# Normalizing with tokens on the partitions: transposes and row statistics in place of matrix products, in a four-layer attention and feed-forward kernel

## The chip, the cores and the metric

One NeuronCore of a Trainium2 chip runs the whole program in one launch. The metric is the device time in microseconds. The engines are PE (TensorE, matrix products; its weight loads are shown apart as PEld), DVE (VectorE), ACT (ScalarE), POOL (GpSimd) and SP (SyncE, which here only issues DMAs). Each engine works through its own instruction queue in order and waits on semaphores that the others raise.

## The reference

The input is 2 batches of 2048 tokens with 128 features. Four blocks follow, each with its own weights, and then an outer norm, a feed-forward part with ternary weights, and a last norm:

```
for i in range(4):
    residual = x
    q, k, v = x @ Wq[i] + bq[i], x @ Wk[i] + bk[i], x @ Wv[i] + bv[i]
    Q, K = elu(q) + 1, elu(k) + 1
    KV, Ksum = sum over tokens of K * v, sum over tokens of K
    V = Q * KV * 1 / (Q * Ksum + 1e-6)
    a = gelu(gelu(V @ Wo[i] + bo[i]))
    x = ln(a + residual) * ln1_s[i] + ln1_b[i]          # norm "1"
    residual = x
    f = gelu(gelu(x @ W1[i] + b1[i]) @ W2[i] + b2[i])    # 128 -> 512 -> 128
    x = ln(f + residual) * ln2_s[i] + ln2_b[i]           # norm "2"
x = layernorm(x_in + x)                                  # norm "x"
h = gelu_exact(x @ ternary(W_fc)); h = layernorm(h) * ln_w + ln_b   # over 512, norm "g"
x = layernorm(x + h @ ternary(W_proj))                   # norm "z"
```

Every norm takes mean and variance over the features of one token.

## The kernel before

Everything on chip is kept transposed: the 128 features lie on the 128 partitions and the tokens run along the free dimension. The 4096 tokens are cut into four pairs of 1024 (`PAIR`, two PSUM banks), two pairs p = 0, 1 for each batch n. PSUM is four tiles of 128x1024, handed out in the fixed order of the list `ORDER` (in the tail `TURNS`).

The work goes in 8 steps (t = 0 to 7; a step is one batch in one layer, batches in turn, so layer 0 is steps 0 and 1), followed by a tail. Step t does the attention of its batch, norm 1 and the up product with its gelu; beside them it does what the step before left over for the other batch: the down product, its gelu and norm 2. So a step waits at its start for the norm 2 that the step before finished last. Matrix products with weights that need more precision are made of three single-pass products (`xh*wh`, `xh*wl`, `xl*wh`: lines 957, 958, 963), where `xh` is x rounded to fp32r and `xl` the remainder. The plain fp32 products show as two records each in the profile (so `x8` for 4 matmuls).

A norm in this layout sums over partitions, which only PE does here:

1. `centered` (L880 for norms 1, x, z; L883 and L885 for norm 2, from `xh`, `xl` of y): the product with I - 1/128 gives y minus its mean in PSUM.
2. ACT squares it (L326) and copies it to `yc` (L327).
3. `mean_rows` (L892): 8 products for a pair with one column of 1/128, in turn in another place of the weights, put the variances of 8x128 tokens into an 8x128 (or 16x128) tile.
4. DVE runs `rsqrt_of` on that tile (L486 to L511, 11 instructions, each waiting for the one before).
5. `spread` (L899): 8 products with `pick` spread the result over all partitions.
6. DVE multiplies with scale and rstd (L693, L680, L518), adds the shift (L699, L682, L524), and `xh` and `xl` are made for the next product (L394, L409, L521 and L533, L298).

The order on PE in a step is: k, v, q products of both pairs; down product of the other batch's pair 0; attention output; half of the down product of pair 1; norm 1 of both pairs with norm 2 of pair 0 between; up products of pair 0; up products of pair 1 with norm 2 of pair 1 between. The tail does norm 2 of the last batch, norm x, the 512-wide hidden layer with the exact gelu (L1122, L1124, L437), its norm g from sums that DVE (L803), ACT (L447) and POOL (L311, L316) make, the projection (L1109) and norm z, for the four pairs, and stores the output transposed back on the host.

SP stores each pair when its norm z is done. POOL makes the remainder `xl` of y (L290) for norm 2 and of x (L298).

## Time and profile before

| | |
|---|---|
| three timed runs | 651.79, 648.50, 651.72 us; median 651.72 |
| span of the profiled execution | 649.9 us (its time outside the span isn't recorded) |
| PE | 570.2 us busy (88%), 2436 matmul records |
| DVE | 460.4 us (71%), 807 instructions |
| ACT | 380.4 us (59%), 371 |
| POOL | 116.6 us (18%), 62 |
| mean granted TensorE clock | 0.967 of full speed |

The span is measured from the first instruction to the last of one execution. Busy time is the sum of the records of an engine. PE records are modelled at their ends and overlap, so the time that a row of matmuls takes is best read from the starts of its rows. In a row of the timeline the number in brackets is the idle time of that engine before it, with what ended it.

### The profile page before, as it was taken

To read this page: it belongs to the slowest core of one execution; us is meant where nothing else is said; L and a number is where in the kernel's file an instruction comes from. 1 tells how busy PE (TensorE), PEld (TensorE's weight loads), DVE (VectorE), ACT (ScalarE), POOL (GpSimd) and SP (SyncE) were. 2 spreads that over 40 slices of the span, in tenths; PEclk is the share of its full clock that TensorE was granted. 3 is DMA by queue.
4 is the path that set the end of the run, shared out by engine and by line. 5 is a ranking of instruction groups with operands and counts; after the bars stand their busy time and mean duration, and the time that the engine had idled before them with its cause. 6 is when DMAs were issued, how large, how long until landed. Compare 5 with 4: busy or idle time off the path is not lost.

```text
span 649.9 us, 7136 instructions
## 1 busy us (share of the span) xinstructions
PE 570.2 (88%) x2436; PEld 358.0 (55%) x2436; DVE 460.4 (71%) x807; ACT 380.4 (59%) x371; POOL 116.6 (18%) x62
## 2 busy tenths in 40 slices
PE   4687989988998899989898988998899989894995
PEld 3345635753674466456645653675366565662554
DVE  6856466886678497758766987579477286989644
ACT  2653774767586747766774777476745348237030
POOL 6200010311021112011300311021110119018000
PEclk9877999999999999999999999999999989997997
DMA  6000100000001000000100000000001010000003
GB/s 210 0 2 0 49 2 0 2 0 1 2 0 49 0 0 0 0 0 0 48 1 0 0 0 0 0 0 0 2 0 66 1 65 2 1 0 2 0 1 129
DMA packets 2756, 10.26 MB, mean 16 GB/s; under 512 B 560, under 2 KB 560, under 8 KB 2480
## 3 DMA queue, kind: packets, MB, share of 16 engines
q1 hardware_dynamic: 2736, 9.99, 4.4%
q8 instruction: 12, 0.20, 0.1%
q14 instruction: 8, 0.07, 0.0%
HBM read 7.90 MB, written 2.10 MB: 15 GB/s over the span
## 4 chain that ended last, share of the span: by engine, by line
PE 49%; DVE 31%; issue 10%; ACT 9%; DMA 0%; DVEq 0%; ACTq 0%; SPq 0%
PE tile L892 13%; PE tile L880 6%; PE tile L899 6%; PE tile L1109 5%; PE tile L957 5%; PE tile L963 4%; PE tile L958 4%; DVE y L712 4%; DVE kk L615 3%; DVE kw L609 3%; DVE a L803 2%; DVE y L624 2%; DVE qw L622 2%; ACT y L348 1%; ACT a L384 1%
## 5 line engine op out<-in xcount | busy, mean ns | idle before, releaser
L957 PE MATMUL tile<-xh,wh 128*128 128x512 f32 x224 | 97.0, 433 | 19.2 <-DVE xh L750 9.5
L984 PE MATMUL tile<-h,w 128*128 128x512 f32 x224 | 101.6, 601 | 4.1 <-ACT a L367 2.0
L290 POOL TENSOR_TENSOR xl<-y,xh 128x1024 fp32r<-128x1024 f32 x16 | 38.1, 2381 | 358.4 <-DVE xh L529 358.4
L963 PE MATMUL tile<-xl,wh 128*128 128x512 f32 x224 | 89.0, 409 | 4.6 <-POOL xl L298 4.6
L958 PE MATMUL tile<-xh,wl 128*128 128x512 f32 x224 | 90.5, 404 | 0.0
L373 ACT ACTIVATE h<-tile,b 128x1024 f32<-128x1024 f32 x64 | 69.5, 1109 | 33.9 <-PE tile L963 33.8
L892 PE MATMUL tile<-sq,slide 128*16 128x128 f32 (+1 forms) x640 | 74.9, 276 | 0.0
L984 PEld LDWEIGHTS tile<-h,w 128*128 128x128 f32 x224 | 40.8, 190 | 56.8 <-issue 48.5
L892 PEld LDWEIGHTS tile<-sq,slide 128*16 128x16 f32 (+1 forms) x640 | 59.6, 95 | 19.3 <-ACT yc L327 5.3
L957 PEld LDWEIGHTS tile<-xh,wh 128*128 128x128 f32 x224 | 43.2, 193 | 44.5 <-issue 14.5
L326 ACT ACTIVATE sq<-tile 128x1024 f32<-128x1024 f32 x40 | 41.3, 1032 | 41.2 <-PE tile L880 37.6
L880 PE MATMUL tile<-y,center 128*128 128x512 f32 x96 | 48.7, 638 | 18.1 <-DVE y L712 15.1
L899 PE MATMUL tile<-rr,pick 48*128 48x128 f32 (+1 forms) x352 | 49.7, 286 | 12.6 <-DVE rr L511 12.5
L899 PEld LDWEIGHTS tile<-rr,pick 48*128 48x128 f32 (+1 forms) x352 | 44.4, 196 | 27.5 <-issue 24.6
L394 ACT ACTIVATE xh<-yc,att 128x512 fp32r<-128x512 f32 (+1 forms) x24 | 20.7, 862 | 57.2 <-DVE yc L693 57.2
L963 PEld LDWEIGHTS tile<-xl,wh 128*128 128x128 f32 x224 | 42.8, 194 | 19.4 <-POOL xl L298 7.3
L958 PEld LDWEIGHTS tile<-xh,wl 128*128 128x128 f32 x224 | 43.5, 194 | 7.3
L486 DVE TENSOR_SCALAR vv<-tile 8x128 f32<-8x128 f32 (+1 forms) x28 | 7.8, 278 | 51.9 <-PE tile L892 51.7
L298 POOL TENSOR_TENSOR xl<-x,xh 128x1024 fp32r<-128x1024 f32 x12 | 30.1, 2512 | 75.7 <-DVE x L524 44.8
L327 ACT ACTIVATE yc<-tile 128x1024 f32<-128x1024 f32 x40 | 41.5, 1038 | 0.0
L880 PEld LDWEIGHTS tile<-y,center 128*128 128x128 f32 x96 | 18.2, 201 | 41.8 <-issue 39.8
L712 DVE TENSOR_TENSOR y<-a,x 128x1024 f32<-128x1024 f32 x16 | 34.0, 2158 | 6.6 <-ACT a L384 5.6
(138 smaller groups left out, 927.1 us busy)
## 6 DMA issues: line engine op xcount, KB each, us to landing
raw<-layers SPq DMA_DIRECT2D x3, 774.5 KB, 4.2
x<-x_t SPq DMA_DIRECT2D x4, 512.0 KB, 6.7
y<-x_t SPq DMA_DIRECT2D x2, 1024.0 KB, 5.1
out_t<-x SPq DMA_DIRECT2D x4, 512.0 KB, 2.6
raw<-layers SPq DMA_DIRECT2D x1, 512.0 KB, 7.6
raw<-layers SPq DMA_DIRECT2D x1, 256.0 KB, 2.6
sq<-fc_t SPq DMA_DIRECT2D x1, 256.0 KB, 7.1
sq<-proj_t SPq DMA_DIRECT2D x1, 256.0 KB, 7.3
```

The source lines that it names most:

```text
L290: pool.tensor_tensor(xl[:, c], y[:, c], xh[:, c].bitcast(F32), ALU.subtract).then_inc(y_lo["2"], 1)
L326: act.activation(squares_of[k][:, p, :], tile[slot][:, :], ACT.Square).then_inc(sq_ready[k], 1)
L327: act.activation(yc[:, cols(n, p)], tile[slot][:, :], ACT.Copy).then_inc(yc_ready[k], 1)
L373: act.activation(h[:, p, j * PAIR:(j + 1) * PAIR], tile[slot_of(("h", p, j))][:, :], ACT.Gelu_apprx_tanh, bias=b1[:, j:j + 1]).then_inc(h_ ...
L712: dve.tensor_tensor(y[:, cols(n, p)], a1[:, p, :], x[:, cols(n, p)], ALU.add).then_inc(y_ready["1"], 1)
L880: mm = pe.matmul(dst, center[:, :].bitcast(F32), y[:, c], start=True, stop=True)
L892: mm = pe.matmul(dst, weights[:, at:at + rows], src[:, r * ROW:(r + 1) * ROW], start=first and r == 0, stop=last and r == ROWS_PER_PAIR - 1)
L899: mm = pe.matmul(tile[slot][:, r * ROW:(r + 1) * ROW], pick[0:LOW + rows, row0 + r, :], rr, start=True, stop=True)
L957: pe.matmul(dst, wh[:, w0:w0 + P], xh[:, c], start=True, stop=False)
L958: pe.matmul(dst, wl[:, w0:w0 + P], xh[:, c], start=False, stop=False)
L963: mm = pe.matmul(dst, wh[:, w0:w0 + P], xl[:, c], start=False, stop=True)
L984: mm = pe.matmul(dst, w2[:, j * P:(j + 1) * P], h[:, p, j * PAIR + at:j * PAIR + at + BANK], start=(j == 0), stop=(j == FT - 1))
```

## The change

In all norms the tokens go to the partitions. `turned` transposes eight 128x128 blocks of a pair with PE's transpose into PSUM (identity as the moving operand). In that layout a token's 128 features lie in one partition's row: DVE takes `bn_stats` of each block (8 instructions of 128 columns for a pair), and `moments` makes mean, variance, 1/sqrt and -mean/sqrt for the 8 blocks at once with 16 small instructions of 128x8 elements. The normalized rows `nt` are made from PSUM block by block (128x128) by DVE (`rows_normed`, subtract and multiply) or ACT (Identity with scale and bias), transposed back by PE, and scale and shift of the norm are applied on the way out of PSUM by ACT (for pair 1 of norm 2 by DVE). The squares, the products with `center`, `slide` and `pick`, and the POOL work for y are gone. PSUM slots are given out by the lists `USERS`.

In the tail the hidden layer comes out in rows as well: `hidden(m)` makes 256 tokens x 512 features with the tokens on the partitions (16 chunks, m = 0 to 15), ACT applies the exact gelu into `hd`, DVE takes `bn_stats` of 512 columns twice, `hidden_turned` transposes 8 blocks back for the projection (128x128 products), and the projection comes out in rows. Its norm's 1/sqrt is then a scalar for each row, applied in `final_sum` with the residual rows `nt` (to which POOL has added the constant part, `with_constant`). Norm z needs no transposes, and the output is stored in rows in eight pieces of 512 columns. The last norm 2 is applied together with the sum for norm x (`outer_sum`), for which POOL adds the shift to the input (`shifted`).

```
...
-TURNS += [("rf", 3), ("cz", 1), ("vz", 0), ("cz", 2), ("cz", 3), ("rz", 0), ("rz", 1), ("vz", 1), ("rz", 2), ("rz", 3)]
-LAST = [key for key in TURNS if key[0][-1] != "+"]
+MEAN, RSTD, SHIFT, VAR, A, B, C = range(7)
+NCOLS = 7
+MOMENT_STEPS = 16
+HIDDEN_STEPS = 13
+NEWTON_SCALE = 0.375 ** 0.2
+
+
+USERS = [[("k", 0), ("v", 1), ("o", 1), ("n2", 0), ("h", 1, 2)],
+         [("v", 0), ("q", 1), ("n1", 0), ("h", 0, 1), ("h", 0, 3), ("h", 1, 1)],
+         [("q", 0), ("f", 0), ("f", 1), ("h", 0, 0), ("h", 0, 2), ("h", 1, 0), ("h", 1, 3)],
+         [("k", 1), ("fold", 0), ("o", 0), ("n1", 1), ("n2", 1)]]
+OF_STEP_BEFORE = ("f", "n2")
+CHUNKS = FT
 
 
...
-            def squares(k, slot, n, p, done, reuse=None):
-
-                act.wait_ge(c_mm[k], done + 1)
-                if reuse is not None:
-                    act.wait_ge(var_mm[k], reuse)
-                act.activation(squares_of[k][:, p, :], tile[slot][:, :], ACT.Square).then_inc(sq_ready[k], 1)
-                act.activation(yc[:, cols(n, p)], tile[slot][:, :], ACT.Copy).then_inc(yc_ready[k], 1)
+            def affine(dst, src, scale, shift, done):
+                act.activation(dst, src, ACT.Identity, bias=shift, scale=scale).then_inc(done, 1)
+
+            def rows_normed(k, slot, n, p, q, rows):
+
+                for r in rows:
+                    last = act.activation(nt[:, row_cols(n, p, r)], tile[slot][:, r * P:(r + 1) * P], ACT.Identity,
+                                          bias=value(k, q, SHIFT, r), scale=value(k, q, RSTD, r))
+                last.then_inc(n_act[k], 1)
...
+            def moments(k, q, call, eps, width=P):
+
+                base = call * MOMENT_STEPS
+                done = moment[k]
+                even, odd, even2, odd2 = (stats[k][:, q, :, c] for c in (1, 4, 2, 5))
+                mean, shift, rstd, v, a, b, c = (value(k, q, z) for z in (MEAN, SHIFT, RSTD, VAR, A, B, C))
+                dve.wait_ge(stats_ready[k], call + 1)
+                dve.tensor_tensor(a, even, odd, ALU.subtract).then_inc(done, 1)
+                dve.tensor_tensor(b, even2, odd2, ALU.add).then_inc(done, 1)
+                dve.tensor_tensor(mean, even, odd, ALU.add).then_inc(done, 1)
+                dve.wait_ge(done, base + 1)
+                dve.scalar_tensor_tensor(a, a, 0.25, a, ALU.mult, ALU.mult).then_inc(done, 1)
+                dve.wait_ge(done, base + 2)
+                dve.tensor_scalar(b, b, 1.0 / width, eps, ALU.mult, ALU.add).then_inc(done, 1)
+                dve.wait_ge(done, base + 3)
+                dve.tensor_scalar(mean, mean, 0.5, None, ALU.mult).then_inc(done, 1)
+                dve.wait_ge(done, base + 5)
+                dve.tensor_tensor(v, a, b, ALU.add).then_inc(done, 1)
+                rsqrt_of(k, q, base + 7)
+                dve.wait_ge(done, base + 15)
+                dve.scalar_tensor_tensor(shift, mean, -1.0, rstd, ALU.mult, ALU.mult).then_inc(done, 1)
+
+            def row_stats(k, q, slot):
+                for r in range(ROWS):
+                    last = dve.bn_stats(stats[k][:, q, r, :], tile[slot][:, r * P:(r + 1) * P])
+                last.then_inc(stats_ready[k], 1)
+
+            def rows_normed(k, q, slot, n, p, half):
+                for r in range(half * HALF, (half + 1) * HALF):
+                    last = dve.tensor_scalar(nt[:, row_cols(n, p, r)], tile[slot][:, r * P:(r + 1) * P],
+                                             value(k, q, MEAN, r), value(k, q, RSTD, r), ALU.subtract, ALU.mult)
+                last.then_inc(n_dve[k], 1)
...
                     scaled_projection()
-
-                for p, rows, rr in ((0, ROWS_PER_PAIR, rr2[:, 0, :]), (1, ROWS, rr1)):
-                    dve.wait_ge(var_mm["1"], 2 * t + p + 1)
-                    rsqrt_of("1", 2 * t + p, tile[slot_of(("v1", p))][0:rows, 0:ROW], rows, rr[0:rows, :],
-                             rr[LOW:LOW + rows, :], BLOCK_EPS)
-
-                first_scaled(0, 0, BANK)
-                first_shifted(0, 0, BANK, 0)
-                first_scaled(0, BANK, BANK)
+                first_moments(0)
+                first_rows(0, 0)
+                first_moments(1)
                 first_low(0, 0, BANK, 0)
-                first_shifted(0, BANK, BANK, 1)
+                first_rows(1, 0)
+                first_rows(1, 1)
                 first_low(0, BANK, BANK, 1)
                 if left:
                     second_sum(1)
-                first_scaled(1, 0, PAIR)
-                first_shifted(1, 0, PAIR, 2)
+                    second_moments(0)
+                    second_rows(0, 0)
+                    second_rows(0, 1)
                 first_low(1, 0, PAIR, 2)
+                if last:
+                    outer_sum(0)
                 if left:
-                    second_norm(0)
                     if n == 1 and next_layer is not None:
                         take_attention(next_layer)
-                    second_rsqrt()
...
+            def turned(slot, src, n, p, rows):
+
+                for r in rows:
+                    mm = pe.transpose(tile[slot][:, r * P:(r + 1) * P], src[:, row_cols(n, p, r)], ident[:, :])
                 return mm
 
...
+                def first_turned(p):
+                    slot = free(("n1", p))
+                    pe.wait_ge(y_ready["1"], 2 * t + p + 1)
+                    turned(slot, y, n, p, range(ROWS)).then_inc(t_mm["1"], 1)
+
+                def first_back(p):
+                    slot = slot_of(("n1", p))
+                    for half in range(2):
+                        if p == 0 and half == 1:
+                            pe.wait_ge(n_act["1"], t + 1)
+                        else:
+                            pe.wait_ge(n_dve["1"], 3 * t + 1 + p * (half + 1))
+                        turned(slot, nt, n, p, range(half * HALF, (half + 1) * HALF)).then_inc(back_mm["1"], 1)
+
...
-                    weight_sums(free(("c2", 0)))
-                first_centered(0)
+                    weight_sums(free(("f", 0)))
+                first_turned(0)
+                first_turned(1)
                 if left:
-                    second_centered(0)
-                first_centered(1)
-                if not left:
-                    projected_ln_b(free(("f", 1)))
-                first_variance(0)
-                first_variance(1)
-                first_rstd(0)
-                if left:
+                    second_turned(0)
                     down(1, 1)
                 else:
-                    first_rstd(1)
+                    projected_ln_b(slot_of(("f", 0)))
+                first_back(0)
                 up(0, [0, 1])
-                if left:
-                    first_rstd(1)
                 up(0, [2])
+                first_back(1)
                 up(0, [3])
                 if left:
-                    second_centered(1)
-                    second_rstd(0)
+                    second_back(0)
                 up(1, [0])
                 if left:
-                    second_variance()
+                    second_turned(1)
                 else:
-                    projection_means(free(("v2", 1)))
+                    projection_means(free(("n2", 1)))
                 up(1, [1])
                 up(1, [2])
                 up(1, [3])
                 if left:
-                    second_rstd(1)
+                    second_back(1)
 
...
+            def hidden_turned(m):
+                if m == 0:
+                    pe.wait_ge(xx_lo, 2)
+                else:
+                    pe.wait_ge(g_ready, m)
+                pe.wait_ge(d_ready, m + 1)
+                for z in range(ROWS):
+                    mm = pe.transpose(tile[3][:, z * P:(z + 1) * P], hd[:, m % 3, z * P:(z + 1) * P], ident[:, :])
+                mm.then_inc(g_mm, 1)
...
```

How the instructions of a step stand on the queues. PE, before, from the first half of the other batch's second down product to its second half (tile is PSUM, sq the squares, rr the 1/sqrt rows):

```order
L984 MATMUL tile<-h,w 128x512 x4
L880 MATMUL tile<-y,center 128x512 x2
L883 MATMUL tile<-xh,center 128x512
L885 MATMUL tile<-xl,center 128x512
L883 MATMUL tile<-xh,center 128x512
L885 MATMUL tile<-xl,center 128x512
L880 MATMUL tile<-y,center 128x512 x2
L892 MATMUL tile<-sq,slide 8x128 x8
L892 MATMUL tile<-sq,slide 16x128 x16
L1020 REGISTER_ALU
L899 MATMUL tile<-rr,pick 128x128 x8
L984 MATMUL tile<-h,w 128x512 x4
```

The same place on PE in the changed kernel, up to the first up product (nt are the normalized rows):

```order
L932 MATMUL tile<-h,w 128x512 x4
L855 MATMUL tile<-ident,y 128x128 x24
L932 MATMUL tile<-h,w 128x512 x4
L959 ISA
L855 MATMUL tile<-ident,nt 128x128 x8
L156 REGISTER_ALU x2
L905 MATMUL tile<-xh,wh 128x512
```

The 24 transposes of y (pairs 0 and 1 for norm 1, pair 0 for norm 2) now stand together, the rest of the down product comes behind them, and only then the 8 transposes back, which wait for the normalized rows of pair 0.

DVE, before, from the end of the second 1/sqrt of norm 1 to the remainder of pair 0:

```order
L511 SCALAR_TENSOR_TENSOR rr<-ry,rr 16x128
L693 SCALAR_TENSOR_TENSOR yc<-yc,att,tile 128x512
L698 ISA
L699 TENSOR_SCALAR x<-yc,att 128x512
L693 SCALAR_TENSOR_TENSOR yc<-yc,att,tile 128x512
L533 TENSOR_TENSOR xl<-x,xh 128x512
L698 REGISTER_ALU
L699 TENSOR_SCALAR x<-yc,att 128x512
L533 TENSOR_TENSOR xl<-x,xh 128x512
```

DVE in the changed kernel, first from the end of the moments of pair 0 (norm 1) into those of pair 1:

```order
L493 REGISTER_ALU
L494 SCALAR_TENSOR_TENSOR work<-work 128x8
L503 TENSOR_SCALAR nt<-tile,work 128x128 x4
L498 BN_STATS stats<-tile 128x6 x8
L481 TENSOR_TENSOR work<-stats 128x8
L482 TENSOR_TENSOR work<-stats 128x8
```

and then from the end of the moments of pair 1 to the statistics of norm 2:

```order
L494 SCALAR_TENSOR_TENSOR work<-work 128x8
L653 ISA
L655 TENSOR_TENSOR xl<-x,xh 128x512
L503 TENSOR_SCALAR nt<-tile,work 128x128 x8
L653 REGISTER_ALU
L655 TENSOR_TENSOR xl<-x,xh 128x512
L630 REGISTER_ALU
L631 TENSOR_TENSOR y<-a,x 128x1024
L498 BN_STATS stats<-tile 128x6 x8
```

The remainder of the first half of pair 0 (L655), which the first up product waits for, now stands behind the whole statistics and moments of pair 1; before, both 1/sqrt chains stood ahead of it.

## Rows read from the trace of the kernel before

**Rows 1.** Busy time by stretch: us, each engine's busy time and count, clock, DMA.
```profile
133.70:194.30 60.60, 56.49 (x240) 35.15 (x239) 44.71 (x79) 41.47 (x41) 9.53 (x4) 1.00 0.00 1
499.70:557.00 57.30, 51.09 (x201) 29.62 (x200) 36.75 (x45) 30.62 (x33) 20.53 (x8) 0.97 0.06 19
```

**Rows 2.** The chain that ended last, in order of time: start, us, what.
```profile
37.09 6.71 PE tile L880 x8
...
155.99 3.38 DVE y L712
...
191.55 1.09 PE tile L899 x8
...
499.73 7.06 PE tile L1109 x16
```

**Rows 3.** PE groups of the norms between 133.7 and 194.3 us.
```profile
L880 PE MATMUL tile<-y,center 128*128 128x512 f32 x8 | 3.8, 602 | 1.9 <-DVE y L712 1.9
L892 PE MATMUL tile<-sq,slide 128*8 128x128 f32 x32 | 3.8, 273 | 0.0
...
L892 PE MATMUL tile<-sq,slide 128*16 128x128 f32 x32 | 3.7, 272 | 0.0
...
L899 PE MATMUL tile<-rr,pick 40*128 40x128 f32 x16 | 2.2, 276 | 0.0
L883 PE MATMUL tile<-xh,center 128*128 128x512 f32 x4 | 2.0, 494 | 0.0
L885 PE MATMUL tile<-xl,center 128*128 128x512 f32 x4 | 1.6, 395 | 0.0
```

**Rows 4.** Timeline of DVE in step 2: start, us, line, what.
```profile
153.90 1.22 DVE L663 TENSOR_TENSOR y<-a,x 128x1024 f32<-128x1024 f32 x1 [2.54 <-ACT a L367]
...
169.49 0.28 DVE L486 TENSOR_SCALAR vv<-tile 16x128 f32<-16x128 f32 x1 [0.20 <-PE tile L892]
...
172.80 0.75 DVE L693 SCALAR_TENSOR_TENSOR yc<-yc,att,tile 128x512 f32<-128x512 f32 x1
...
195.97 2.34 DVE L561 COPY outp<-raw 128x3 f32<-128x3 f32 x1
198.88 0.69 DVE L609 TENSOR_SCALAR kw<-kw 128x1024 f32<-128x1024 f32 x1 [0.58 <-DVE outp L561]
```

**Rows 5.** Timeline of DVE: dependent and independent small instructions.
```profile
44.77 0.87 DVE L592 TENSOR_SCALAR pw<-pw,ffn_norm 128x128 f32<-128x128 f32 x4
...
146.50 0.16 DVE L639 RECIPROCAL fold<-fold 128x1 f32<-128x1 f32 x1
146.70 0.16 DVE L641 TENSOR_TENSOR fold<-fold 128x1 f32<-128x1 f32 x1
```

**Rows 6.** Timeline of ACT in step 2.
```profile
156.99 1.06 ACT L384 ACTIVATE a<-a 128x1024 f32<-128x1024 f32 x1
...
165.13 1.06 ACT L326 ACTIVATE sq<-tile 128x1024 f32<-128x1024 f32 x1
166.03 1.07 ACT L327 ACTIVATE yc<-tile 128x1024 f32<-128x1024 f32 x1
173.58 0.72 ACT L394 ACTIVATE xh<-yc,att 128x512 fp32r<-128x512 f32 x1 [6.48 <-DVE yc L693]
```

**Rows 7.** ACT group of the same line on 1024 columns, 133.7 to 194.3 us.
```profile
L394 ACT ACTIVATE xh<-yc,att 128x1024 fp32r<-128x1024 f32 x1 | 1.2, 1154 | 0.5 <-DVE yc L693 0.5
```

**Rows 8.** Timeline of POOL in step 2.
```profile
155.93 2.35 POOL L290 TENSOR_TENSOR xl<-y,xh 128x1024 fp32r<-128x1024 f32 x1 [18.36 <-DVE xh L529]
```

**Rows 9.** Timeline of PE in step 2.
```profile
153.92 3.70 PE L984 MATMUL tile<-h,w 128*128 128x512 f32 x8 [0.35 <-ACT a L367]
...
175.40 0.72 PE L963 MATMUL tile<-xl,wh 128*128 128x512 f32 x2
```

**Rows 10.** Busy time by stretch in the tail.
```profile
592.00:596.00 4.00, 0.00 (x0) 0.00 (x0) 3.90 (x2) 4.00 (x5) 3.86 (x2) 0.59 0.00 2
596.00:600.00 4.00, 2.24 (x11) 1.45 (x12) 4.00 (x2) 0.54 (x1) 3.67 (x2) 0.50 0.02 4
```

**Rows 11.** DMA issues: name, count, KB each, us to landing.
```profile
out_t<-x SPq DMA_DIRECT2D x4, 512.0 KB, 2.6
```

972 lines of the change are left out of this document (482 added, 490 removed), and 3 rows, old and new, of the table ORDER.

## The prediction

> **What bounds the kernel now.** I read the busy time by stretch first: a steady step takes 60.6 us, and of it PE is busy 56.5, DVE 44.7, ACT 41.5 [rows 1]. That is PE at 93%, so it looks bound by PE. The chain in order of time says otherwise: it goes from engine to engine. In step 2 it waits for DVE's sum y (3.38 us), passes the variance products, ends with the spread at 191.55 [rows 2], and the next step's keys start on DVE at 198.88 [rows 4]. Two waits make it long: the sum y takes 3.38 us where the same sum takes 1.22 [rows 2, 4], because POOL works on the remainder of y from 155.93 to 158.28 [rows 8]; and the norm 1 takes from the sum at 155.99 to the first scaled half at 172.80 [rows 2, 4], with DVE idle for part of it. PE fills this time with the norm's own products. So the step is a chain through the norms, and I work out the change along it.
>
> **What is removed.** In a step PE loses 3.8 + 3.8 + 3.7 + 2 x 2.2 + 2.0 + 1.6 = 19.3 us of records [rows 3] (L899 has a second group of the same count and time; some overlap, so about 17 us of time). ACT loses 8 instructions of 0.90 (start to start [rows 6]), 7.2 us. DVE loses three 1/sqrt chains of 3.3 us (172.80 less 169.49 [rows 4]), two casts of y, and the scaling in two passes. POOL loses its two remainders of y, 2.35 each [rows 8], and with the first the 2.2 us that DVE waited for it.
>
> **What is added, with prices.**
> - 64 transposes of 128x128 a step. No row shows one. The nearest is L899, 128-column weights and 128 moving columns in one pass: 2.2 us for 16, 0.14 each [rows 3]; the upper end is two passes, 0.28, and no gain below about 0.11 is likely, since a two-pass 128-column product takes 3.8/32 = 0.12 for a pass. I take 0.13, 8.3 us a step.
> - 32 bn_stats and 28 row instructions of 128 columns on DVE. Four independent 128-column instructions take 0.87 us, 0.22 each [rows 5]; waiting for each other they take 3.31/11 = 0.30 [rows 4]. I take 0.235 (1.9 us for eight), with 0.20 and 0.30 as ends.
> - Four sets of moments, 16 instructions of 8 columns each. Dependent ones of one column start 0.20 apart [rows 5]. Eleven of the 16 stand in one dependent line, the rest goes between: 2.4 us a set. At the 0.30 of the 128-column chain it would be 4.8, the upper end.
> - On ACT 4 row instructions in norm 1 of pair 0. From 0.72 us at 512 columns and 1.154 at 1024 the slope is 0.85 ns a column [rows 6, 7], so 128 columns take 0.39; I let the second per-row operand and the overlap of 0.16 that rows 6 show cancel: 0.38 a piece. Besides, x is now made by ACT as well as xh (another 0.72 + 0.72 + 1.15 + 1.15).
>
> The Trainium skill (VectorE: DVE Perf Modes, The TRN2 errata) says that a source in PSUM costs 120 + columns cycles at 0.96 GHz and that small tiles pay the fixed part each time, which speaks against cutting 1024 columns into eights. By it a 128-column piece is 0.26 us. That is not far from the 0.22 of rows 5; with 0.26 the forecast would come out about 1.5 us a step, 12 us in all, later.
>
> **The step walked through**, on the clock of step 2 of before (attention's second gelu of pair 0 ends when the sum of 155.99 starts). Sum y(0) ends at 157.2 instead of 159.4. PE is in the down product until 157.6 [rows 9], then transposes pair 0 until 158.7. DVE does sum y(1) (its gelu ends at 158.05 [rows 6]) to 159.3, then, without a pause: statistics of pair 0 to 161.2, moments to 163.6, four rows to 164.6 (ACT the other four to 165.3), statistics and moments of pair 1 to 168.9, and only then the remainder of the first half, to 169.6. PE has pairs 0, 1 and norm 2's pair 0 transposed by 161.5, the down product's rest until 165.0, pair 0 turned back by 166.1. The first xh is ready at 167.1, but the up product needs the remainder too: 169.6 against 175.4 before [rows 9]. From there DVE stays the longest line: rows of pair 1 to 171.5, second remainder 172.2, sum 173.4, norm 2 of pair 0 (4.3 + 1.9) 179.6, remainder of pair 1 180.8, wait for the transposes until 183.0, statistics and moments of norm 2's pair 1 to 188.0 (0.7 of it waiting for POOL's remainder, as the 2.34 us for three columns show [rows 4]), rows to 189.9. PE turns back until 190.4 and starts the next step's keys there, 192.6 before (191.55 + 1.09 [rows 2]). DVE makes x and xh of pair 1 until 192.5, POOL its remainder in 2.4 us until 194.9, and the keys on DVE, 198.88 before [rows 4], start at about 195.0. So a steady step gets 3.9 us shorter, 56.7 us, and DVE rather than PE is what it waits for. In the steps that take the next attention weights, that copying falls into the wait before 183.0.
>
> Six steps (1 to 6) give 6 x 3.9 = -23.4. Step 7 counts up to the tail's first product, 191.5 + 1.1 before and 189.7 now: -2.8. Step 0 has no norm 2, and DVE's ternary weights stand ahead of the statistics: the second remainder comes 1.8 us later than before and the up products follow: +1.5.
>
> **The tail.** Before it runs from 499.7 to 649.9, 150.2 us [rows 2]. Now, from its first product: the two down products (6.9 each, from 7.06 for 16 records [rows 2]) interleaved with three norms in sequence, each transposes 1.1, moments 4.3, eight ACT rows 3.1, back 1.1: the first exact gelu starts 32.7 us in. Chunks 0 to 8, in which the four remaining norm chains and the first final sums sit between the chunks on all engines and hold PE up by 3 to 6 us each, take 51.5. Chunks 9 to 15: PE has 0.93 for the four products, 1.05 for 8 transposes, 8 x 0.23 = 1.8 for the projection, 3.8 in all; DVE has statistics, final sums and moments of 3.9 on average, so 4.1 each, 28.7. Then 7.6 for the last transposes and projections, and 10.3 at the end: final sums 2.0, moments 2.4, eight ACT rows 3.1, the DMA 2.6 [rows 11]. Together 130.8: -19.4.
>
> Two costs come on top. Where PE had been idle for 4 us the granted clock went to 0.59 and then 0.50 (1.2 GHz) and the next products took place there [rows 10]; at that level 8 records of the centring product take 6.71 us, at full speed 3.8 [rows 2, 3]. The first half of the new tail has such gaps, 6 us the longest; I take four bursts of 2 us longer: +8. POOL has 8 instructions of up to 2.4 us there that hold DVE as above: +3.
>
> Sum: 649.9 - 23.4 - 2.8 + 1.5 - 19.4 + 8 + 3 = 616.8. The profiled span is 1.8 under the median of the runs, 651.7; with that 618.6, and I forecast 618.
>
> **The rivals.**
> - *Slower: the transposes don't keep the clock up.* Between 157.6 and 169.6 PE would do 32 transposes, waits, and one 3.5 us piece of real products. If the granted clock falls in each step there, that piece takes 3.5 more and each of the 48 up products 0.2 more (half speed, from 0.23), 13 us, of which the gaps take up some 5. That is +7.5 a step over my forecast, 7 steps, 53: 671. It decides from 4.7 us a step (33/7), half of the up products at 1.2 GHz. Against it: the profile keeps 1.00 throughout the steps [rows 1]; for it: that was with PE at 93%. The Trainium skill (TensorE: Matmul & The Clock Gate, Part 4: PE-mode transpose) says just this, that transposes don't count as busy, and gives about 275 ns for one; no row here shows a transpose.
> - *No gain: DVE's pieces cost what dependent ones cost* (0.30 for statistics and rows): 60 x 0.065 = 3.9 a step eats the gain, 27 in the steps and 7 in the tail: 652.
> - *Half of it: the tail is held longer.* Every burst of its first half at 1.2 GHz and the handovers 1 us longer each: +18, 636.
> - *More: no clock loss in the tail, no POOL collisions, pieces at 0.20 to 0.22*: -8, -3, -9: 598.
>
> **How the numbers follow.** Forecast (606 to 630) 0.50, more 0.17, half 0.17, no gain 0.08, slower 0.08. All but the last two are faster; of the no-gain case (645 to 660) a fifth is faster, two fifths unchanged and two fifths slower, where 0.5% (3 us) is about what a measurement can tell. Faster 0.86, same 0.03, slower 0.11. The range leaves out the slower case and the outer parts of the others: 597 to 645; the likeliest case alone is 606 to 630.
>
> **What would show it.** A transposed block of 0.13 us, bn_stats of 128 columns at 0.235 start to start and a set of moments in 2.4; the sum y(0) at 1.22; steps of 56 to 57 us with PE near 48 busy and DVE at 46 to 50; the first up product waiting for the remainder (L655), not for xh; clock 1.00 through the steps and under 1 in the first half of the tail; a tail of about 140. It would be wrong if the clock falls in the steps, if the moments are over 3.5 us, or if the chunks after the eighth take more than 5 us.

## The result and the profile after

The changed kernel takes 654.42 us (median of 5 runs, 652.6 to 657.8), the kernel before 650.31 (5 runs). The ratio is 1.0072, interval 1.0043 to 1.0101: a little slower, where 618 us was forecast. Against the forecast for the profiled run (span 616.8) the measured span is 653.3, so 36.5 us are to be explained. Where they lie, by the first product of the tail and by what follows it (us of the profiled runs):

| | before | forecast | after |
|---|---|---|---|
| mean of steps 1 to 6 | 61.1 | 57.2 | 62.0 |
| first product of the tail | 499.7 | 475.0 | 505.5 |
| from there to the end | 150.2 | 141.8 | 147.8 |

So 30.5 us are missing ahead of the tail (28.7 in steps 1 to 6 and 2.0 in step 7; step 0 is 0.2 better than forecast) and 6.0 in the tail. The page of the changed kernel (busy us, share, instructions; then the granted clock in 40 slices) shows a first difference:

```profile
PE 492.6 (75%) x2052; PEld 338.0 (52%) x2052; DVE 469.6 (72%) x1609; ACT 373.2 (57%) x433; POOL 51.2 (8%) x32
...
PEclk9767998999888979996879789999999976878898
```

Step 2 and the start of the tail by stretch, to be laid beside [rows 1] (us, busy time and count of each engine, clock, DMA):

```profile
133.35:194.76 61.41, 50.06 (x191) 31.83 (x190) 48.76 (x159) 38.84 (x40) 4.80 (x2) 0.94 0.00 1
505.51:563.00 57.49, 38.33 (x157) 26.20 (x157) 33.08 (x110) 23.11 (x44) 9.27 (x5) 0.77 0.06 19
```

TensorE lost 6.4 us of busy time in the step and is at 50 where 48 was forecast, VectorE gained 4.0 and is at 49, inside the forecast's 46 to 50. The clock was 1.00 there, now 0.94; in the tail 0.97 has become 0.77. The step is no shorter.

VectorE in step 2 of the changed kernel (start, us, line, what, idle time before). It is to be read against the forecast's walk, whose clock is 1.0 us later:

```profile
154.98 1.22 DVE L671 TENSOR_TENSOR y<-a,x 128x1024 f32<-128x1024 f32 x1 [0.87 <-ACT a L333]
...
158.22 1.68 DVE L498 BATCH_NORM_STATS2 stats<-tile 128x6 f32<-128x128 f32 x8
...
162.61 1.36 DVE L503 TENSOR_SCALAR nt<-tile,work 128x128 f32<-128x128 f32 x4
...
168.12 0.69 DVE L655 TENSOR_TENSOR xl<-x,xh 128x512 fp32r<-128x512 f32 x1
168.72 2.64 DVE L503 TENSOR_SCALAR nt<-tile,work 128x128 f32<-128x128 f32 x8
...
183.59 1.68 DVE L498 BATCH_NORM_STATS2 stats<-tile 128x6 f32<-128x128 f32 x8 [2.37 <-PE tile L855]
185.31 1.45 DVE L481 TENSOR_TENSOR work<-stats 128x8 f32<-128x8 f32 x1
...
189.01 2.64 DVE L503 TENSOR_SCALAR nt<-tile,work 128x128 f32<-128x128 f32 x8
192.85 1.34 DVE L701 TENSOR_SCALAR x<-tile,outp 128x1024 f32<-128x1024 f32 x1 [1.21 <-PE tile L855]
...
195.18 2.39 DVE L531 COPY outp<-raw 128x3 f32<-128x3 f32 x1
201.34 0.69 DVE L580 TENSOR_SCALAR kw<-kw 128x1024 f32<-128x1024 f32 x1 [3.77 <-issue]
```

Up to the end of the first remainder (168.8; forecast 169.6, less 1.0) the walk holds to 0.2 us: the sum of pair 0 is 1.22 us where it was 3.38 [rows 2], the statistics 0.21 each. After it each block of eight row pieces (L503) takes 2.64 us, 0.33 a piece, where 1.9 was forecast, and the last set of moments (from 185.31) takes 3.7 where the others take 2.4 to 2.7: its first instruction, 0.17 us elsewhere, takes 1.45 beside POOL's remainder of x (184.32 to 186.72). The last rows end at 191.65, 2.8 later than forecast. The four transpositions behind them run at half clock:

```profile
191.70 1.11 PE L855 MATMUL tile<-ident,nt 128*128 128x128 f32 x4 [0.16 <-DVE nt L503]
```

That makes it 3.5 at the start of L701. And the keys of the next step, forecast for 195.0, which is 194.0 here, start at 201.34 behind 3.77 us in which VectorE waits for nothing that the trace shows. So the 7.3 us at the end of the walk are 2.8 on VectorE, 0.7 at half clock, 3.7 of this wait and 0.1 more. The same place in the chain of waits, at the end of steps 2, 4 and 6 (start, us, what):

```profile
197.75 3.46 issue
...
325.10 3.70 issue
...
450.35 0.05 issue
```

The loop has three passes of two steps, so it turns back twice, behind steps 2 and 4, and is left behind step 6. The wait stands at the two turns and not at the exit. Step 1 lasts 58.4 us; steps 3 and 5, which begin with the turn, last 65.8 and 65.4.

TensorE in step 2 shows the clock (a product record of 512 columns is 0.4 us at 2.4 GHz, 0.63 at 1.2):

```profile
164.02 1.09 PE L855 MATMUL tile<-ident,nt 128*128 128x128 f32 x8 [0.21 <-DVE nt L503]
167.96 0.50 PE L905 MATMUL tile<-xh,wh 128*128 128x512 f32 x1 [2.84 <-ACT x L264]
...
172.01 0.74 PE L911 MATMUL tile<-xl,wh 128*128 128x512 f32 x2 [1.45 <-DVE xl L655]
173.72 0.80 PE L905 MATMUL tile<-xh,wh 128*128 128x512 f32 x1 [0.97 <-ACT h L314]
174.31 0.63 PE L906 MATMUL tile<-xh,wl 128*128 128x512 f32 x1
```

Eight transpositions take 1.09 us, 0.13 each, as forecast. Then TensorE waits 2.84 us, not for the remainder (L655) but for x of the second half (L264): the first two up products go together, and the second of them is written into the very tile that ScalarE is still reading. It still starts 0.6 us ahead of the forecast's 168.6. Waits and transpositions follow each other, and from 173.7 to 176.9 the up products are at half clock; the next ones, from 177.4 on, are at full clock again:

```profile
176.44 1.18 PE L855 MATMUL tile<-ident,nt 128*128 128x128 f32 x8
177.38 0.48 PE L905 MATMUL tile<-xh,wh 128*128 128x512 f32 x1
177.70 0.39 PE L906 MATMUL tile<-xh,wl 128*128 128x512 f32 x1
```

I measure the clock's loss as the sum over stretches of 4 us, from 72 to 468 us, of (1 - granted clock) x 4, in us of full speed, rounded. Before it is 0. After it is 29. It is read from one execution each, and it varies: e4 below, whose steps are those of the changed kernel, lost 22. The gelus of the tail's chunks (ScalarE):

```profile
543.56 1.02 ACT L378 ACTIVATE hd<-tile 128x1024 f32<-128x1024 f32 x1
...
600.19 1.02 ACT L378 ACTIVATE hd<-tile 128x1024 f32<-128x1024 f32 x1 [3.72 <-PE tile L1070]
603.78 1.02 ACT L378 ACTIVATE hd<-tile 128x1024 f32<-128x1024 f32 x1 [1.65 <-PE tile L1070]
607.38 1.02 ACT L378 ACTIVATE hd<-tile 128x1024 f32<-128x1024 f32 x1 [0.75 <-PE tile L1070]
...
615.28 3.18 ACT L396 ACTIVATE x<-y,work_z 128x128 f32<-128x128 f32 x8 [5.96 <-DVE work_z L494]
618.37 1.00 ACT L378 ACTIVATE hd<-tile 128x1024 f32<-128x1024 f32 x1
```

Chunk 0 starts 38.1 us into the tail (forecast 32.7 without its two charges, 8 for the clock and 3 for POOL). The next 56.6 us, to the start of chunk 8, are taken against the forecast's 51.5 for chunks 0 to 8, the 36.4 from there to the start of chunk 15 against its 28.7 for chunks 9 to 15, and 16.7 are left for the end (17.9). The first two are 10.5 over, about what the 11 us of charges were put down for; the later chunks are 7.7 over, and those nothing in the forecast covers. Between chunks 10 and 11 lie 11.0 us where others lie 3.6 apart: ScalarE stands ahead of the final rows of block 1 for 5.96 us.

### The profile page after: what moved, and what is told of

Its sections match the earlier page's. It is cut to its first block, busy times and chain, and to the rows that moved or that the text cites. A ratio compares the mean times of both kernels' runs of the same rounds, so it can differ in the third digit from the quotient of the medians.

```text
span 653.3 us, 7183 instructions
## 1 busy us (share of the span) xinstructions
PE 492.6 (75%) x2052; PEld 338.0 (52%) x2052; DVE 469.6 (72%) x1609; ACT 373.2 (57%) x433; POOL 51.2 (8%) x32
## 4 chain that ended last, share of the span: by engine, by line
DVE 46%; PE 27%; ACT 16%; issue 10%; DMA 1%; DVEq 0%; ACTq 0%; SPq 0%
DVE nt L503 9%; DVE stats L498 7%; PE tile L855 5%; PE tile L905 3%; PE tile L911 3%; PE tile L932 3%; PE tile L906 3%; ACT nt L269 2%; DVE kk L586 2%; ACT a L333 2%; ACT a L330 2%; PE tile L1025 2%; PE tile L945 2%; PE tile L1093 2%; DVE y L595 2%
## 5 line engine op out<-in xcount | busy, mean ns | idle before, releaser
L855 PE MATMUL tile<-ident,nt 128*128 128x128 f32 x288 | 50.6, 323 | 50.9 <-DVE nt L503 33.0
L855 PEld LDWEIGHTS tile<-ident,nt 128*128 128x128 f32 x288 | 39.4, 166 | 67.9 <-DVE nt L503 46.4
L503 DVE TENSOR_SCALAR nt<-tile,work 128x128 f32<-128x128 f32 x208 | 68.9, 406 | 0.0
L498 DVE BATCH_NORM_STATS2 stats<-tile 128x6 f32<-128x128 f32 x256 | 53.8, 288 | 13.2 <-PE tile L855 13.1
L269 ACT ACTIVATE nt<-tile,work 128x128 f32<-128x128 f32 x48 | 17.8, 460 | 58.7 <-DVE work L494 58.7
L855 PE MATMUL tile<-ident,y 128*128 128x128 f32 x288 | 37.3, 278 | 13.8 <-DVE y L671 8.8
L855 PEld LDWEIGHTS tile<-ident,y 128*128 128x128 f32 x288 | 32.9, 143 | 22.3 <-issue 15.7
L761 DVE BATCH_NORM_STATS2 stats_g<-hd 128x6 f32<-128x512 f32 x32 | 20.5, 684 | 21.5 <-ACT hd L378 21.4
L264 ACT ACTIVATE xh<-tile,att 128x512 fp32r<-128x512 f32 (+1 forms) x24 | 22.4, 935 | 21.1 <-PE tile L855 21.1
L945 PE MATMUL tile<-y,wo_kv 128*128 128x512 f32 x64 | 31.4, 636 | 3.1 <-DVE bias_o L616 3.1
```

Of the source, the lines that this page charges most:

```text
L264: act.activation(dst, src, ACT.Identity, bias=shift, scale=scale).then_inc(done, 1)
L269: last = act.activation(nt[:, row_cols(n, p, r)], tile[slot][:, r * P:(r + 1) * P], ACT.Identity, bias=value(k, q, SHIFT, r), scale=value( ...
L498: last = dve.bn_stats(stats[k][:, q, r, :], tile[slot][:, r * P:(r + 1) * P])
L503: last = dve.tensor_scalar(nt[:, row_cols(n, p, r)], tile[slot][:, r * P:(r + 1) * P], value(k, q, MEAN, r), value(k, q, RSTD, r), ALU.sub ...
L855: mm = pe.transpose(tile[slot][:, r * P:(r + 1) * P], src[:, row_cols(n, p, r)], ident[:, :])
L945: mm = pe.matmul(dst, wo_kv[:, :], s[:, part(n, p, at)], start=True, stop=True)
```

## The experiments

All runs as ratios to the kernel before, each against runs of it on the same chip; "lost" is the clock's loss as defined above, "step" the mean of steps 1 to 6. The last three columns are of the one profiled execution. e7 and e11 leave the scaling out of the rows, so their times are prices and not those of a kernel to be used.

| kernel | us | ratio (interval) | step | lost | first tail product |
|---|---|---|---|---|---|
| after | 654.4 | 1.0072 (1.0043 to 1.0101) | 62.0 | 29 | 505.5 |
| e1 after, loop written out | 639.3 | 0.9824 (0.9774 to 0.9874) | 59.2 | 15 | 489.8 |
| e2 before, loop written out | 649.2 | 0.9976 (0.9950 to 1.0002) | 61.0 | 0 | 497.8 |
| e3 after, turned by products | 670.4 | 1.0284 (1.0219 to 1.0348) | 63.0 | 12 | 516.5 |
| e4 after, tail's gelus first | 647.5 | 0.9939 (0.9904 to 0.9974) | 62.1 | 22 | 506.8 |
| e5 e1 + rows on ScalarE | 638.0 | 0.9807 (0.9780 to 0.9833) | 59.5 | 26 | 488.7 |
| e6 e1 + TensorE kept busy | 636.9 | 0.9795 (0.9760 to 0.9829) | 59.1 | 3 | 487.8 |
| e7 e1 + constants in rows | 631.8 | 0.9696 (0.9674 to 0.9717) | 58.9 | 25 | 485.1 |
| e8 e5 + e6 + e4 | 613.3 | 0.9412 (0.9367 to 0.9457) | 57.2 | 0 | 472.7 |
| e9 after, VectorE written out | 643.5 | 0.9878 (0.9837 to 0.9919) | 59.9 | 22 | 495.3 |
| e10 after, others written out | 652.6 | 1.0033 (1.0009 to 1.0057) | 61.4 | 27 | 501.5 |
| e11 e6 + e7 | 619.6 | 0.9519 (0.9502 to 0.9536) | 56.7 | 0 | 469.7 |
| e12 e8 + chunk 5 first | 611.5 | 0.9391 (0.9373 to 0.9408) | 57.2 | 0 | 474.5 |

### The turn of the loop

**e1 and e2: the loop written out.** On every engine:

```diff
-            with dve.Fori(0, LAYERS - 1) as i:
+            for i in range(0, LAYERS - 1):
```

> The changed kernel with its loop over three pairs of steps written out (all five engines), nothing else. Theory L (the turn of the loop costs: VectorE stands 3.77 us at 197.6 and 4.02 at 324.9 us with the keys' input ready, nothing at the loop's end at 450.3, and steps 3 and 5 last 65.8 and 65.4 us where step 1 lasts 58.4): steps 3 and 5 fall to 58.5 to 61.5, in all 9 to 14 us less, 640 to 646 us. Rival C (the stall is only a part, the low granted clock of TensorE in the steps makes the rest): only the stall itself goes, 3.5 twice, steps 3 and 5 stay at 61.5 to 62.5, 647 to 649 us. Rival N (the time without a cause in the record is a wait for something in the kernel, or code that has to be fetched whatever its form): no change, 652 to 657.

> The kernel before with the same loop written out. In it steps 3 and 5 last 62.4 us, step 1 60.1, and VectorE shows 0.58 us without a cause at the turn. Theory L: 2.3 us a turn at most, 645 to 649 us, so that the loop's turn takes some 5 us more from the changed kernel than from this one. Rival: the turn costs this kernel nothing, 650 to 652. If code written out has to be fetched everywhere: slower, 652 to 660.

The changed kernel gets 2.5% faster, 16 us by the ratios (15.2 by the medians), the kernel before 0.2%, whose interval reaches to no change. Theory L holds and goes a little beyond what it expected: steps 3 and 5 last 58.1 and 61.6 us. It is more than the two stalls of 3.5 and 3.7. A part of the rest is clock: the loss is 15 for 29, of which 7 can be the variation between executions, but the mean granted clock of all four and five executions says the same (0.907 for 0.893 over the whole span). That a stall alone brings such a loss shows in e13 below: 7 us, all of them in the 16 us from the start of each of its two stalls, in a kernel that without them loses none.

**e9 and e10: on which engine.** The same edit on VectorE alone, and on all others alone.

> The changed kernel with the loop written out on VectorE alone; the other engines loop as before. Theory V (it is VectorE's own turn that costs: its loop body has grown by 188 instructions to more than before, and the 3.5 us stand on VectorE with its input ready): the gain of e1 comes whole, 638 to 642 us against 654.4 with the loop everywhere. Rival G (the turn of any engine costs and VectorE only shows it; or the clock after the turn's wait makes it): half or less of the gain, 645 to 652.

> The complement: the loop written out on TensorE, ScalarE, GpSimd and SyncE, and kept on VectorE. Theory V: VectorE still stands 3.5 us at each of two turns, and the time is 650 to 655 us. Rival G: some 640 to 648.

Ratios 0.9878 (0.9837 to 0.9919) and 1.0033 (1.0009 to 1.0057): from 1.0072 that is 12.6 and 2.5 us. Most of it is VectorE's turn, a little less than theory V's "whole" (643.5 us for 638 to 642); a small part, just at the edge of the intervals, belongs to the others, and why was not looked into. With the others written out VectorE still stands 4.0 and 4.4 us at the turns. (The loop body on VectorE has 419 instructions after and 241 before, 178 more and not the 188 named there. These are counts of the program. The traces hold 441 and 271 records of VectorE's queue for a pass, 170 more, and 449 in e13, 345 in e15 and e16.)

**e13 to e16: what makes the turn dear.** The queue of the program's code, in the kernel before and in the changed one (queue: packets, MB, share):

```profile
q14 instruction: 8, 0.07, 0.0%
```

```profile
q14 instruction: 24, 0.20, 0.1%
```

The kernel before gets tiny instructions on VectorE, 89 a step in e13 and e14, 37 in e15 and e16, and in e16 100 more ahead of the loop; e14 is e13 with the loop written out.

```diff
                 constant_part()
+                for j in range(89):
+                    dve.memset(pad[:, n * 90 + j:n * 90 + j + 1], 0.0)
```

> The kernel before with 89 writes of one column to an unused buffer on VectorE in each step, so that its loop body there has 241 + 178 = 419 instructions like the changed kernel's. They take some 0.07 us each beside a wait of 2.5, so the steps get longer by 3 to 5 us each whatever the theory. Theory B (the body's size makes the turn dear): q14 moves 24 to 28 packets in place of 8, VectorE stands 3 to 4 us without a cause at each of the two turns, and the kernel is 8 to 16 us slower than its form with the loop written out (e14). Rival O (it is something else of the changed kernel, such as what stands around the turn): no such wait, and within 2 us of e14.

> The same padding with the loop written out on all engines: the control for e13. By theory B 8 to 16 us faster than e13, by rival O the same within 2.

> The kernel before with 37 one-column writes to an unused buffer on VectorE in each step: a loop body of 315 instructions, which begins after 124. Theory W (the turn is dear when its target lies too far back: e13's body of 419 began after about 176 and ended at 595, the changed kernel's runs from 123 to 542, the kernel before's from 87 to 328; at 439 the start is still held): no wait at the turn, q14 8 to 12 packets, 649 to 653 us. Theory L (a body of over 256 instructions is too long wherever it lies): a wait of about 3.5 us at each turn, q14 17 packets or more, 655 to 659.

> The same loop body of 315 instructions, with 100 more of these writes in step 0, so that it runs from 224 to 539. The 100 take some 7 us of step 0's time if nothing hides them. Theory W with fixed blocks of code (the target is lost when the body ends in a third block of 256): a wait of about 3.5 us at each of two turns and q14 17 packets or more, where e15 has none, and 12 to 16 us more than e15. Theory W by distance alone (315 back in both) or theory L: the same at the turn as e15, and at most 7 us more.

| | body | ratio (interval) | q14 packets | step 3 |
|---|---|---|---|---|
| before | 241 | 1 | 8 | 62.4 |
| e13 | 419 | 1.0090 (1.0058 to 1.0123) | 21 | 64.3 |
| e14, written out | none | 0.9976 (0.9952 to 1.0000) | 17 | 62.1 |
| e15 | 315 | 1.0083 (1.0050 to 1.0116) | 20 | 65.7 |
| e16, 100 later | 315 | 1.0110 (1.0060 to 1.0160) | 20 | 65.5 |

The padding itself costs nothing (e14 has the ratio of e2, so the 3 to 5 us a step expected for it did not come). With the loop it costs 7.4 us against e14 and 5.9 against the kernel before, a little under the 8 to 16 of theory B, with 21 packets for 24 to 28. VectorE shows the changed kernel's wait in e13:

```profile
200.19 0.69 DVE L610 TENSOR_SCALAR kw<-kw 128x1024 f32<-128x1024 f32 x1 [3.38 <-issue]
```

So nothing of the norms is needed for the wait: a longer loop body is enough. The price is not the same, though: 5 to 7 us in the kernel before (e13, e15, e16), 13 to 16 in the changed one (e9, e1); the lost clock is a part of the difference, and the rest is open. A body of 315 has the wait as one of 419 (3.8 and 3.9 us in e15, 3.4 and 3.7 in e16; the profile puts some of them down to ScalarE's kw, which had been done before the wait began), in both places tried, so theory W falls in both forms that I gave it; the limit lies between 241 and 315 instructions, and where was not tried. The Trainium skill (Runtime: NRT & Kernel Launch, Instruction fetch mechanics) says that a taken branch whose target is no longer in a window of two blocks of 256 instructions forces a fetch of its block. The traces agree with the stall at the branch and with added packets: 24 in the changed kernel where it has 16 with VectorE's loop written out (e9), so 4 a turn. But neither way to read "two blocks" fits all runs. If the last two run through are meant, e15, from instruction 124 to 439, should have escaped the stall, and did not; if the present one and the next, the kernel before, from 87 to 328, should have had it, and has 0.58 us.

### The clock and the row pieces

**e3: the norms' transpositions as float32 products.**

```diff
-                    mm = pe.transpose(tile[slot][:, r * P:(r + 1) * P], src[:, row_cols(n, p, r)], ident[:, :])
+                    mm = pe.matmul(tile[slot][:, r * P:(r + 1) * P], src[:, row_cols(n, p, r)], ident[:, :],
+                                   start=True, stop=True)
```

> The changed kernel with every transposition of the norms (64 a step, and those of the norms in the tail; the hidden rows are still turned as before) issued as an ordinary float32 product with the identity. A float32 product of 128 columns takes 0.11 us in the last part (16 in 1.79), a transposition 0.13, so the instruction itself is no dearer. Theory T (the transpositions do not hold the clock up): the granted clock in the steps is back at 1.00, steps 2 and 4 fall from 61.4 and 62.7 to about 58.4, 640 to 648 us. Rival W (the clock falls because TensorE waits longer in the steps, whatever it issues): the granted clock falls in the same windows, 652 to 657. Rival S (a float32 product of 128 columns with a new stationary operand each time is dearer here): 64 times more than 0.13, above 657.

Theory T has the direction of the clock: the loss falls from 29 to 12 us, not to none, and 5 of the 12 lie in the two stretches of 16 us that begin with the waits at the turns. Rival S is right on the price: eight take 1.95 us (two records each), 0.24 and not 0.11, and the kernel is slower. The expectation's 0.11 was the time of one record, of which a product has two. The longer products also leave TensorE less time to wait (between 72 and 260 us it is busy 166.2 us, and 151.5 in the changed kernel), so e3 does not tell whether the transposition as such fails to hold the clock or the wait beside it lets it fall: rival W is weakened, not excluded. In the kernel before, small products of the norms stood in this place and the clock stayed at 1.00, with TensorE busy 56.5 of 60.6 us [rows 1].

```profile
110.29 1.95 PE L855 MATMUL tile<-ident,nt 128*128 128x128 f32 x16
```

**e5: eight row pieces a step moved to ScalarE.** Pair 1 of the first norm, behind `first_out(0, BANK, BANK, 2)`, on top of e1:

```diff
+                act.wait_ge(moment["1"], (2 * t + 2) * MOMENT_STEPS)
+                rows_normed("1", slot_of(("n1", 1)), n, 1, 1, range(ROWS))
...
-                first_rows(1, 0)
-                first_rows(1, 1)
```

> The changed kernel with the loop written out, and in every step the eight row pieces of the first norm's second pair on ScalarE (from tile's rows, behind the first pair's results) in place of VectorE. Theory D (VectorE sets the length of a step: it is busy 2.7 to 3.0 of every 3 us from the first sums to the next keys, and its row pieces take 0.33 us each, not the 0.235 forecast; ScalarE stands idle there from 169.7 to 175 us): VectorE loses 8 x 0.33 = 2.6 us a step, 12 to 18 us in seven steps, 621 to 628 us against 639.3. Rival C (the clock of TensorE and the wait for the first up product set it): VectorE only waits longer, 636 to 640. Rival A (ScalarE comes late with the gelus behind the rows): 640 to 648.

**e6: TensorE kept busy.** On top of e1:

```diff
+                def kept_busy(slot, count):
+                    for _ in range(count):
+                        pe.matmul(tile[slot][:, 0:P], ident[:, :], ident[:, :], start=True, stop=True)
...
                 first_back(0)
+                kept_busy(free(("h", 0, 0)), 6)
                 up(0, [0, 1])
...
+                    ge(pe, *emptied(t, ("h", 1, 2)))
+                    kept_busy(0, 8)
                     second_back(1)
```

> The changed kernel with the loop written out, and in every step 14 float32 products of the identity with itself (0.24 us each, results never read) in two stretches in which TensorE only waits: six ahead of the first up product, eight ahead of the second norm's last transpositions. Theory C (a wait among transpositions drops the clock to 1.2 GHz, which slows the up products at 168 to 175 us and the first key products at 192 to 195): the granted clock stays at 1.00 in the steps and each step gets 1 to 2 us shorter, 627 to 634 us against 639.3. Rival D (VectorE sets the step's length and the products at half clock only use up slack): the clock is 1.00 and the time falls by less than 4 us, 636 to 640. Rival: the products delay what they stand ahead of, 640 to 646.

**e7: the price of a piece.** On top of e1, in `rows_normed` on VectorE:

```diff
-                                             value(k, q, MEAN, r), value(k, q, RSTD, r), ALU.subtract, ALU.mult)
+                                             0.5 if k == "1" else value(k, q, MEAN, r),
+                                             1.0, ALU.subtract, ALU.mult)
```

> The changed kernel with the loop written out, its row pieces on VectorE changed to find their price: those of the first norm take two constants, those of the second one value per row and a constant, in place of two values per row (the scaling is left out of the computation). Theory P (each per-row operand costs): 0.33 us becomes about 0.24 with constants and 0.28 with one, 11 to 14 us less in all if VectorE sets the steps, 625 to 632. Rival Q (the price is that of PSUM to SBUF in 128 columns, whatever the operands): 0.33 in all three, 638 to 641.

The rows of e7 answer the question of the price: with two constants eight pieces take 1.66 us, with one per-row operand 2.15, with two (above) 2.64. That is 0.21, 0.27 and 0.33 a piece, so each such operand costs 0.06.

```profile
168.79 1.66 DVE L503 TENSOR_SCALAR nt<-tile 128x128 f32<-128x128 f32 x8
...
176.24 2.15 DVE L503 TENSOR_SCALAR nt<-tile,work 128x128 f32<-128x128 f32 x8
```

In time each of the three alone disappoints. e5 takes 2.6 us a step from VectorE and gains 1 us in all by the ratios, which is not clear of noise: theory D falls as stated. e6 holds the clock (3 us lost) and gains 2 us, as its rival D said, also within the intervals. e7 gains 7.5, where P expected 11 to 14 (its 631.8 us is at the upper edge of P's 625 to 632). But e5 and e7 lose 26 and 25 us of clock where e1 lost 15. By the mean clock of the whole span in all four executions of each (0.899 and 0.902 against 0.907) the difference is smaller, 5 and 2 us of full speed.

**e11: both at once.**

> The changed kernel with the loop written out, constants in the row pieces of the first norm and one value a row in those of the second (the scaling is left out), and the 14 products a step that keep TensorE busy. Alone, the products took 2.4 us away (e6, which has the clock at 1.00 almost throughout the steps) and the cheaper pieces 7.5 (e7, in which the clock lost 26 us worth of full speed in the steps, 7 more than in e1). Theory S (the two hide each other: a step is as long as the later of VectorE and of the half-clock products, so that a cheaper VectorE only brings more low clock): together more than the sum of 10, namely 13 to 20 us, 619 to 626. Rival (they add up): 628 to 631.

| | TensorE as it is | kept busy |
|---|---|---|
| two per-row operands | 639.3 (e1) | 636.9 (e6) |
| one or none | 631.8 (e7) | 619.6 (e11) |

Alone they take 7.5 and 2.4 us, together 19.7: theory S, at the good end. Each hides the other. (The 26 and "7 more" of the expectation are 25 and 10 more by the measure of the table.) The steps are 56.7 us long. e11's step 2, and e8's (us, busy, clock):

```profile
130.87:187.61 56.74, 50.42 (x220) 32.90 (x219) 45.16 (x159) 38.95 (x41) 4.81 (x2) 1.00 0.00 1
```

```profile
131.39:188.60 57.21, 50.31 (x220) 33.02 (x219) 45.38 (x151) 41.73 (x49) 4.80 (x2) 1.00 0.00 1
```

Why the clock falls somewhat more when VectorE is faster was not tested apart.

### The order in the tail

**e4: the gelus ahead of the final rows,** ScalarE alone, the loop kept:

```diff
-            final_rows(1)
             hidden(11)
             turned(10)
             hidden(12)
             turned(11)
+            final_rows(1)
...
-            final_rows(2)
             hidden(15)
             turned(14)
             turned(15)
+            final_rows(2)
```

> The changed kernel with another order on ScalarE alone in the tail: the final rows of block 1 behind the gelu of chunk 12 instead of ahead of chunk 11, those of block 2 behind everything else instead of ahead of chunk 15. Theory O (the written order holds the chunks: the gelu of chunk 11 starts 11.0 us after that of chunk 10 and that of chunk 15 starts 6.6 after 14, where others lie 3.6 apart, since ScalarE stands ahead of the final rows until their moments are done): 5 to 9 us less, 645 to 650. Rival (TensorE's own work or the low clock sets the pace there, the waiting only moves, and the rows come late at the end): within 2 us, 652 to 657.

Theory O: the ratio falls by 0.0133, 8.6 us; the steps are as before and the tail lasts 140.2 us for 147.8. Chunk 11 now follows 4.6 us behind chunk 10, and from chunk 8 to chunk 15 lie 26.2 us for 36.4.

```profile
609.14 1.02 ACT L378 ACTIVATE hd<-tile 128x1024 f32<-128x1024 f32 x1 [0.74 <-PE tile L1070]
...
613.77 1.02 ACT L378 ACTIVATE hd<-tile 128x1024 f32<-128x1024 f32 x1 [2.70 <-PE tile L1070]
```

**e8: together,** and **e12** with chunk 5 (product, gelu and turning back) ahead of the last rows of block 3 on TensorE and ScalarE.

> The changed kernel with the loop written out, the first norm's second pair's row pieces on ScalarE, the 14 products a step that keep TensorE busy, and ScalarE's tail with the gelus ahead of the final rows. If the four add up: 639.3 - 7 (tail) - 14 (rows) - 3 (clock): 612 to 620 us. If rows and clock share one slack: 620 to 630. If only the tail's order adds: 630 to 634.

> The combined kernel e8 with one more change of order in the tail: chunk 5 (its product, its gelu and its turning back) ahead of the last rows of the second norm's block 3, on TensorE and ScalarE. In e8 the gelus of chunks 4 and 5 lie 10 us apart, with the moments, rows and transpositions of that block between them. Theory O: the chunk goes into that wait, 3 to 5 us less, 608 to 611 us. Rival (what follows needs that block's results at once, so the wait only moves to a later chunk): 612 to 616.

e8 is 6% faster than the kernel before, 41 us faster than the changed one. It falls into the range of "the four add up", but not as a sum of what they gave: by the ratios e5, e6 and e4 alone gave 1.1, 1.9 and 8.6 us, together they give 26.8 beyond e1. The excess belongs to rows and clock taken away at once, as in e11: the tail's first product comes 17.1 us earlier than in e1, where e5 and e6 alone bring it forward by 1.1 and 2.0, and the tail is as in e4 (139.6 us for 140.2). e12 is 1.8 us lower, but its interval overlaps with e8's. Its gelus of chunks 5 and 6 now lie 11.8 us apart where those of 4 and 5 had lain 10: most of the wait moved to the next chunk, as the rival said. Most and not all: from chunk 4 to chunk 6 it takes 15.4 us for 18.7, and its tail lasts 135.4 us for 139.6, while its steps begin 1.4 us later than e8's for reasons ahead of the edit. So the trace speaks for a gain of theory O's size and the times do not settle it. e8, or e12, is the version to take.

## Why the prediction was wrong, step by step

The step that failed is the end of the walk through a step: "the keys on DVE ... start at about 195.0. So a steady step gets 3.9 us shorter". On the trace's clock they start 7.3 us late, and the steady step that was to take 56.7 takes 61.4. Three things were wrong in it, and a fourth in the tail. Two of the three signs that the prediction named for being wrong came: the clock falls in the steps (0.94), and the chunks from the eighth on take 5.2 us on average, over its 5. The third, moments over 3.5 us, holds only for the set beside POOL's work (3.7).

1. **The turn of the loop was not in the sum.** The forecast counted what each instruction costs and not that VectorE's loop body grows from 241 to 419 instructions. In the trace before, the keys behind the turn had 0.58 us of idle time [rows 4], and nothing there warned of it. Two turns cost 15 to 16 us with what follows from them (e1; e9 and e10 together 15). The wait itself, 3.5 and 3.7 us, is reproduced with tiny instructions alone (e13, e15).
2. **The clock in the steps.** "Clock 1.00 through the steps" was wrong, the slower rival's condition right: it falls among the transpositions and waits, to half in short stretches. That it is the transpositions and not the waits is made likely by e3, not shown. Its price was not the 7.5 us a step that the rival gave: keeping the clock up gains 2.4 us in all as VectorE stands (e6) and 12.2 with cheaper pieces (e7 to e11), under 2 a step, because in step 2 nine product records ran at half clock and not the 48 of the up products. The Trainium skill (TensorE: Matmul & The Clock Gate, Part 4: PE-mode transpose) says that a transposition does not count as busy in the way that a product does; e3 (29 to 12 us) agrees as far as it goes. The 275 ns that it gives for one of bf16 in a kernel is close to the mean length of a record here (278 ns for those of y, float32) and not the price: eight start 0.13 apart at full clock.
3. **The row pieces were under-priced.** Taken 0.235 from a row with one per-row operand and SBUF as source [rows 5]; measured 0.33. 28 a step times 0.095 is 2.7 us a step. The statistics, priced by the same number, cost 0.21, which gives back 0.8, and a set of moments 2.4 to 2.7 for 2.4, the last one 3.7. The no-gain rival had 0.30 for both, 3.9 us a step against these 1.9, so its 652 us came near the result by luck: the rest was the turn and the clock, which it did not have.
4. **The tail's order.** The forecast took 4.1 us for each of the later chunks from the engines' work and not from ScalarE's written order. The later chunks take 36.4 us for 28.7. Forecast for the whole tail with its charges 141.8, measured 147.8; with the order mended (e4) 140.2.

What held: the first half of the walk, the sum of pair 0 at 1.22 (POOL's work on y is gone), transpositions at 0.13, ScalarE's pieces at 0.36 for 0.38, and a first half of the tail below full clock at about the price put down for it. That the first up product waits for L655 did not hold. Nor did it hold as stated that VectorE and not TensorE sets the new step: e5 takes 2.6 us a step from VectorE, e6 gives TensorE its clock, and neither shortens the step by itself (59.5 and 59.1 for 59.2); both together do (57.2, e8). Three of the prediction's sums are off by little and change nothing: step 7 is -2.9 by its own numbers and not -2.8, the end of the tail 10.1 and not 10.3, the slower rival 8 a step and not 7.5. With points 2 and 3 taken away and the loop written out (e11) a steady step is 56.7 us as in the forecast, and the tail's first product comes at 469.7 for 475.0. That is in part luck: e11's pieces (12 at 0.21 and 16 at 0.27) cost 0.3 us a step more than the forecast's, its statistics 0.8 less. The sum of the misses: 505.5 to 489.8 by the turn, to 469.7 by clock and pieces together, which is 5 more than the 30.5 that were missing, and 6.0 in the tail. Of the 5, 3 are in steps 3 and 5, which the forecast left 1.8 us longer than the others, as they are in the kernel before (62.4), and which e11 does in 57.0; 2 are in step 7.

Points 2 and 3 can't be given shares of their own: the pair is worth 19.7 us and its members 2.4 and 7.5 alone.

## What to carry to other kernels

Count the instructions of every engine's loop body (an instruction here is one on the engine's queue, waits and register work included) before and after a change that cuts work into small pieces, and try the loop written out: here it was worth more than any other single edit. When two limits lie close together (an engine's instructions, another one's clock), take both away in one run before judging either: here they gave 2.4 and 7.5 us alone and 19.7 together. Where an engine's order is written by hand, look for the instruction that stands ahead of ready work because its own input is late.

## What the runs showed of the hardware

- A loop body of 315 or 419 instructions on VectorE costs some 3.4 to 4 us of standing at each turn, with 20 to 24 packets of code in all; one of 241 has 0.6 us and 8 packets (before, e13, e15, e16, after).
- A per-row operand adds 0.06 us to a 128-column instruction from PSUM on VectorE: 0.21 with none, 0.27 with one, 0.33 with two (e7).
- A float32 product with the identity on 128 columns takes 0.24 us where the transposition takes 0.13. With products for transpositions the steps lose 12 us of clock and not 29 (e3). 14 more such products a step, put into waits, hold the clock at 1.00 in e8 and e11 and nearly so in e6 (3 us lost).
- In step 2 of the changed kernel TensorE does nothing from 187.7 to 190.4 us; the granted clock is 1.00 up to there, 0.50 (1.2 GHz) from 190.4 to 193.8 and 1.00 from 193.8 on. In the same place of e6, where eight products fill the wait, it stays at 1.00.
